# A three-set ring of routed rows, zeroed in long packets, with scatter waits per tile group and a rewritten order of steps

## The chip, the cores and the metric

The kernel runs on one NeuronCore of a Trainium2 chip. The metric is the device time of one execution in microseconds (us), lower is better. Engine names as in the profile: PE (TensorE matmul), PEld (its weight loads), DVE (VectorE), ACT (ScalarE), POOL (GpSimd), SP (SyncE, which issues most DMAs; SPq is its queue).

## The reference, cut to what matters

Four residual layers are applied to x of 8 batches x 1024 rows x 128 features, float32:

```
x = x + L0_attn(layernorm(x))   # "A": linear attention, a scan over the 1024 rows of a batch, 16 heads of 8x8 state
x = x + L0_ffn(layernorm(x))    # "B": mixture of 8 experts, 2 per row, hidden size 352
x = x + L1_attn(layernorm(x))   # "C": conv3 + selective state-space scan, 16 states per feature
x = x + L1_ffn(layernorm(x))    # "D": mixture of 8 experts, 2 per row, hidden size 128, and 2 shared experts
```

In both mixtures each row goes to its two best experts, and the two results are added with weights. A, B, C and D need nothing of another batch, so the batches form a pipeline.

## The kernel before, in words

All eight batches of x stay in SBUF. The scans of A and C run on VectorE: for a batch, A has 16 steps `a_outer` (L1454), `a_scan` (L1443), `a_qs` (L1461), and C has 16 steps `c_dbx` (L1511), `c_scan` (L1516), `c_prod` (L1502).

The mixtures are done in nine jobs: B0, B1, B23, B45, D01, B67, D23, D45, D6 (the letter is the layer, the digits are the batches; D of batch 7 is computed densely at the end). A job goes through these steps:

- Prepare: `m_stats`, `m_rstd` (POOL, L840), `m_shift`, and for each half batch (four tiles of 128 rows) `m_norm` (ACT, L1171, writes `xn`), `m_turn`, `m_turned`, `m_hi` (ACT, L1221, first half of the float16 split, writes `xrow`), `m_lo` (DVE, L1376), then `m_logits`, `m_choose`, `m_rank`, and `m_place` (DVE), which gives each row its two slots.
- `m_scatter` (POOL, L867): indirect DMAs, one for each tile of 128 rows and each of its two choices (c = 0, then c = 1), that write `xrow` to the job's row set in DRAM. 16 for a job of one batch, 32 for two.
- Blocks of 256 slots: SP loads the rows (`b_rows`, L750) and the experts' weights (`b_w13`, L732, and `b_w2`, L741), PE multiplies (L909 to L911, L1063), SP stores `outs` (L756).
- `m_gather` (POOL, L886): indirect DMAs that add the outputs into x, again one for each tile and choice.

The next layer's `s_stats` of a batch (or the end of the kernel) waits for its gathers, and `s_rstd` (also POOL, L840) follows on the same engine.

A row set has slots that no row is scattered to, and they are zeroed once, so each set is zeroed by a DMA (L686) from a zeroed tile before its first use. There are six sets, three for B and three for D, used in turn. The zeroed tile is the head of `xn`, so the first `m_norm` (L1188 to L1190) waits until all six sets and the float16 weights of B (`keep`, L717) are written. `m_hi` of a job waits in `all_scattered` for all scatters of all jobs before it, since the job before read the same tile `xrow`.

What each engine does in which order is a string ORDER of 4917 letters (L74). Each letter takes the next step of one chain (`chain`, L427): A the layer A, P preparation of jobs, X scatters, G gathers, C the layer C and its scalars, and so on. All engines run their own steps in this one order. Step numbers below are places in this string, from 0. The step `ready("C")` is the first of chain C. On PE and DVE and on ACT (L1163) it waits for the 13 loads of layer C's weights (L693 to L698).

SP's queue at the head issues, in order: x of batches 0 and 1, A's weights, the float32 expert weights (L677, L679), `zero("B", 0)`, x of batches 2 and 3, C's 13 weights, `zero("B", 1)`, `zero("B", 2)`, x of batches 4 to 7, D's weights, three zeroings for D, and then the steps of ORDER, `keep` first.

Of the kernel before, what the change touches and what calls it, by code (L numbers as in the profile page):

```python
# [13 lines left out]
P = 128  # L14
# [27 lines left out]
class BankUses:  # L42
# [56 lines left out]
    "NKkMGLVpdURVyocKqLxwGsAZbeVNhSZRSTRGMweUpeLqycVKoxwGsAehNeTZMeTqUGSMpRwLKoUVyxLKsGAhNeZeNVZpSRNGSTqZyRoMSsRe"
    "UCewLqGKCVsTCMCUqCwLKCGwTAMVTUoMsALKCUqNoLwVKZGCsACCqSoRwseCCGqNCwZVeCwSRPDGTCCMUCPCLKTCCGPMNPUVePCKLCPPCGCP"  # L100
    "ZCCNSPRCCeVCCPZGCSNPRPCCePPPGTMCPUBKTdPMdUccdbbLKLZNSRZPeNSZReVVNSPRZNSReZTSPMXRUTLMVTxUMNxXLbTZUVMbhNLSUKZX"
    "LVTdVNhSXMpZUdSNpKyLxXyZhccSbXVdxNehbZXSdXpPycpPycPxPhbPudxXlhbpdXvucplycxXyvbhnXnxdabhXpdpycXxcyhbXxdpbXhyc"
    "pdGxychbPRxdRGRPRbhPRPpPdGucPplyPcxyGvbhTnMTduxGhbMlTpUvcGpyLcxyhGnUaUVxMKULTGpLVyhUpNVyZeCSRUeCMKLTCCVUCGGG"
    "NCLGUZUSVRMKLTVUCNeLUGZCCUSVRCKCMGCTCUeLVCLGCCNCGCZeCCSRUCCVGCCUCCUCMKLCLVTCCBNCCCUUGVKUMeCLTccbdVbUddLZUVSN"
    "RMKLVPZxSNRPbheUZTSLURPdUKVMPLpTUexycLVbhNUPZpdUSRVycxKMhPUTbeLpdVycxhbNLUpdUVycKMLUxTehLbZSRVdpNcxyZhbSURUV"
    "dKpUMLyceLVPxNPPhbTZUSURVdKpPyxMcPhbTLUedVpUycLNxVUbZhSMKLTUVdURepLycxVUbhNMKLPZVdpuSRxcyPhbPleTPdvuNlpycZvS"
    "xRnhbneUadUpLycxVUbhUMKLTLVdpNcyxZShbURUMKVLTpxycVhNeUZUSLpUVyMKLxTVuhlevulpUvyLCUCCCUCNCMKLPZSVCeVnPPnCUaCU"
    "PCCCBNLeCUZCSLVPVCCPUCCLCCPXKUCCKCVCUCCNXCLKVCZCCSXKNCZCCSXKeXeCebdXbccedeXdXxhbPxdpGbhycPdpXPycxPhbPXudxlhb"
    "XpdpycXvcxyhbXnuxdXhlbpdXpycvcxyXhbnadxGhbpdRpPycGRPRxcPyRRhbPGPxduPhblTGpMdTPycvpMnGcyxTuhblGxdUvbpKnhUMGLy"
    "cKadTVpUNxGKyMLhTbMcLePVdxGVbUpZUehLyScKGLVNPZVNxSKZhNGZNSSpRRyxcRZRhGeSRpeyGeTMTUMGUpLKTLVyMVKCTGUMCLKVTUMC"  # L110
# [9 lines left out]
    "OJGFQIOJFQIGOJFQIOJGFQIOJFQGIOJFQIOGJFQIOJFQIOJFQGIOJOQQQ"  # L120
# [3 lines left out]
def build(nc, t, out):  # L124
# [36 lines left out]
    ROW_SETS = {"B": 3, "D": 3}  # L161
    NTH = [sum(j[0] == s for j in JOBS[:q]) for q, (s, _) in enumerate(JOBS)]
# [3 lines left out]
    with ctx:  # L166
# [45 lines left out]
        xs_d = {(s, i): dram(f"rows_{s}{i}", [SLOTS, D + 1], F32) for s in "BD" for i in range(ROW_SETS[s])}  # L212
# [75 lines left out]
        zero_rows = xn[:, :, :].rearrange("p j d -> p (j d)")[:, 0:D + 1]  # L288
# [29 lines left out]
        h_ring = [mix2[:, sh_at + i * U_WORDS:sh_at + (i + 1) * U_WORDS] for i in range(RH)]  # L318
        xg = sb("xg", [P, RX, NBT, D + 1])
# [22 lines left out]
        for n, (s, _) in KEEP.items():  # L342
            cols_kept = E * R[s]
            if n in stage_at:
                at = stage_at[n]
            stage[n] = arena_c[:, at:at + cols_kept]
            at += cols_kept
            kept[n] = [mix2[:, kept_at + i * cols_kept // 2:kept_at + (i + 1) * cols_kept // 2].bitcast(F16) for i in range(2)]
            kept_at += cols_kept

# [68 lines left out]
        def ssm(b):  # L419
# [13 lines left out]
                                     [("ready", "D")] * (JOBS[q][0] == "D" and NTH[q] == 0) + prepare(q)],  # L433
# [153 lines left out]
        s_zeroed = {key: sem(f"rows_zeroed_{key[0]}{key[1]}") for key in xs_d}  # L587
# [28 lines left out]
        scattered = sem("rows_scattered")  # L616
# [41 lines left out]
        def _(sp):  # L658
# [19 lines left out]
            for c, (r, rows) in enumerate(CHUNKS["B"]):  # L678
# [4 lines left out]
                         zero_rows[rows:P, 0:D].unsqueeze(1).broadcast_to([P - rows, E, D])).then_inc(s_kept["B"], 16)  # L683
# [15 lines left out]
            for i in range(1, ROW_SETS["B"]):  # L699
                zero("B", i)  # L700
# [1062 lines left out]
```

## Time and profile before

| | before |
|---|---|
| three executions | 1800.45, 1800.25, 1806.42 us, median 1800.45 |
| profiled execution | span 1833.6 us, 29178 instructions, mean clock 0.883 |
| PE busy | 1401.7 us (76% of the span) |
| DVE busy | 1361.4 us (74%) |
| ACT busy | 981.4 us (54%) |
| POOL busy | 929.9 us (51%) |
| chain that ended last | PE 23%, issue 16%, POOL 16%, DVE 15%, ACT 11%, SPq 9%, DMA 7% |
| DMA | 369.53 MB, mean 202 GB/s |

No other time of the profiled execution is given than its span. The span is 33.1 us over the median of the timed executions. Busy time is the time in which an engine executes. The "idle before" of an instruction is the time in which its engine stood idle just ahead of it, and the profile infers who ended that wait.

### The profile page before, as it was taken

To read this page: it belongs to the slowest core of one execution; us is meant where nothing else is said; L and a number is where in the kernel's file an instruction comes from. 1 tells how busy PE (TensorE), PEld (TensorE's weight loads), DVE (VectorE), ACT (ScalarE), POOL (GpSimd) and SP (SyncE) were. 2 spreads that over 40 slices of the span, in tenths; PEclk is the share of its full clock that TensorE was granted. 3 is DMA by queue.
4 is the path that set the end of the run, shared out by engine and by line. 5 is a ranking of instruction groups with operands and counts; after the bars stand their busy time and mean duration, and the time that the engine had idled before them with its cause. 6 is when DMAs were issued, how large, how long until landed. Compare 5 with 4: busy or idle time off the path is not lost.

```text
span 1833.6 us, 29178 instructions
## 1 busy us (share of the span) xinstructions
PE 1401.7 (76%) x9192; PEld 943.1 (51%) x9192; DVE 1361.4 (74%) x2543; ACT 981.4 (54%) x1663; POOL 929.9 (51%) x571
## 2 busy tenths in 40 slices
PE   6674899988999789688578567787836776767668
PEld 3342577755776556555355434565613553435345
DVE  6793969788997889649586588288759579639836
ACT  2213262638756666378264554677446575477332
POOL 1000422385451856828838588400278737852875
PEclk9886899999999999989889579889969788879879
DMA  9995373757884669858477678888468767876952
GB/s 238 162 184 116 90 208 119 212 137 249 281 263 137 215 218 292 230 145 281 148 213 169 185 231 220 231 291 281 125 200 247 200 202 250 225 209 210 287 111 50
DMA packets 320067, 369.53 MB, mean 202 GB/s; under 512 B 33801, under 2 KB 260521, under 8 KB 319657
## 3 DMA queue, kind: packets, MB, share of 16 engines
q1 hardware_dynamic: 277672, 336.05, 62.8%
q0 software_dynamic: 42240, 31.61, 9.6%
q8 instruction: 74, 1.21, 0.3%
q14 instruction: 81, 0.66, 0.1%
HBM read 306.09 MB, written 63.42 MB: 202 GB/s over the span
## 4 chain that ended last, share of the span: by engine, by line
PE 23%; issue 16%; POOL 16%; DVE 15%; ACT 11%; SPq 9%; DMA 7%; another core or an unknown queue 1%; POOLq 0%; DVEq 0%; ACTq 0%
POOL x L886 7%; POOL rows_D L867 5%; PE bank L991 3%; DVE arena_c L1516 3%; POOL rows_B L867 2%; PE bank L1063 2%; SPq L664 2%; SPq L686 2%; DVE arena_c L1502 2%; DMA x<-outs,slot_idx 2%; DMA arena_c<-bc_rows 2%; DVE arena_c L1511 2%; PE bank L1098 2%; DVE arena_a L1443 1%; PE bank L951 1%
## 5 line engine op out<-in xcount | busy, mean ns | idle before, releaser
L886 POOL DMA_INDIRECT x<-outs,slot_idx x240 | 465.4, 1939 | 205.2 <-issue 110.7
L991 PE MATMUL bank<-arena_c,ident 128*128 128x512 f32 x512 | 289.2, 702 | 96.9 <-DVE arena_c L1502 95.9
L1516 DVE TENSOR_TENSOR_SCAN arena_c<-arena_c 128x1024 f32<-128x1024 f32 x128 | 292.1, 2283 | 1.8
L909 PE MATMUL bank<-xT_ring,mix 128*128 128x128 f16 (+1 forms) x1296 | 240.9, 225 | 58.0 <-DVE mix L1688 16.7
L910 PE MATMUL bank<-xT_ring,mix 128*128 128x128 f16 (+1 forms) x1296 | 240.4, 225 | 0.0
L911 PE MATMUL bank<-xT_ring,mix 128*128 128x128 f16 (+1 forms) x1296 | 240.3, 225 | 0.0
L1063 PE MATMUL bank<-mix 128*128 128x128 f32 (+1 forms) x1296 | 192.2, 295 | 60.4 <-ACT yrow L1319 36.2
L1063 PEld LDWEIGHTS bank<-mix 128*128 128x128 f32 (+1 forms) x1296 | 172.9, 205 | 96.0 <-issue 86.0
L991 PEld LDWEIGHTS bank<-arena_c,ident 128*128 128x128 f32 x512 | 104.9, 222 | 218.9 <-DVE arena_c L1502 121.7
L867 POOL DMA_INDIRECT rows_D<-xrow,slot_idx x112 | 187.7, 1676 | 40.1 <-issue 30.1
L867 POOL DMA_INDIRECT rows_B<-xrow,slot_idx x128 | 182.2, 1423 | 46.0 <-issue 35.0
L1274 ACT ACTIVATE arena_c<-arena_c,A_w 128x1024 f32<-128x1024 f32 x128 | 145.2, 1147 | 84.2 <-DVE arena_c L1516 82.4
L909 PEld LDWEIGHTS bank<-xT_ring,mix 128*128 128x128 f16 (+1 forms) x1296 | 139.8, 108 | 91.5 <-issue 59.0
L942 PE MATMUL bank<-arena_a,Wv 128*128 128x512 f32 x256 | 148.9, 665 | 43.8 <-DVE arena_a L1454 30.0
L1319 ACT ACTIVATE yrow<-bank,xg 128x128 f32<-128x128 f32 x312 | 97.3, 364 | 135.3 <-PE bank L1063 116.5
L1511 DVE TENSOR_TENSOR arena_c<-arena_c 128x1024 f32<-128x1024 f32 x128 | 154.8, 1213 | 18.7 <-DMA arena_c<-bc_rows 18.7
L1502 DVE TENSOR_TENSOR arena_c<-arena_c 128x1024 f32<-128x1024 f32 x128 | 153.8, 1213 | 8.5 <-DMA arena_c<-bc_rows 8.0
L951 PEld LDWEIGHTS bank<-Wo,arena_a 128*128 128x128 f32 x1024 | 137.3, 205 | 39.9 <-issue 22.5
L1298 ACT COPY xT_ring<-bank 128x512 f16<-128x512 f16 x156 | 90.5, 580 | 114.4 <-PE bank L1038 64.9
L910 PEld LDWEIGHTS bank<-xT_ring,mix 128*128 128x128 f16 (+1 forms) x1296 | 139.5, 108 | 20.3 <-issue 19.7
L951 PE MATMUL bank<-Wo,arena_a 128*128 128x128 f32 x1024 | 143.2, 290 | 6.7 <-DVE arena_a L1461 6.3
L911 PEld LDWEIGHTS bank<-xT_ring,mix 128*128 128x128 f16 (+1 forms) x1296 | 139.6, 108 | 0.0
(225 smaller groups left out, 2460.4 us busy)
## 6 DMA issues: line engine op xcount, KB each, us to landing
arena_c<-bc_rows SPq DMA_DIRECT2D x256, 512.0 KB
mix<-weights_B SPq DMA_DIRECT2D x168, 352.0 KB
mix<-weights_B SPq DMA_DIRECT2D x168, 192.0 KB
outs<-yrow SPq DMA_DIRECT2D x156, 128.0 KB
mix<-weights_D SPq DMA_DIRECT2D x144, 128.0 KB
xg<-rows_B SPq DMA_DIRECT2D x84, 129.0 KB
xg<-rows_D SPq DMA_DIRECT2D x72, 129.0 KB
mix<-weights_D SPq DMA_DIRECT2D x144, 64.0 KB
```

Source lines behind the costliest of these rows:

```text
L867: pool.indirect_dma_start(out=xs_d[s, NTH[q] % ROW_SETS[s]], out_offset=bass.IndirectOffsetOnAxis(ap=slot_idx[:, q % RJ, c, j:j + 1], axis=0),
L886: pool.indirect_dma_start(out=x[:, b, j, :], out_offset=None, in_=y_d[q], in_offset=bass.IndirectOffsetOnAxis(ap=slot_idx[:, q % RJ, c, i ...
L909: pe.matmul(o, hi, xh, start=True, stop=False)
L910: pe.matmul(o, hi, xl, start=False, stop=False)
L911: return pe.matmul(o, lo, xh, start=False, stop=True)
L942: filled(f"A{b}.v{k}", pe.matmul(fill(f"A{b}.v{k}"), Wv[:, f, :], half(normA, h), start=True, stop=True))
L951: last = pe.matmul(bank[A_BANKS[1]][:, rows], qs[:, k % RQ, rows], Wo[:, f, :], start=(f == 0 and j == 0), stop=(f == EF - 1 and j == TH - 1))
L991: last = pe.matmul(bank[C_BANKS[h]][:], ident[:], half(hb[:, n % RR, :], h), start=(n == 0), stop=(n == NS - 1))
L1063: last = pe.matmul(o[:, j * P:(j + 1) * P], h_ring[n % RH][0:rows, at:at + P], w2(q, k, j)[0:rows, c, :], start=(c == 0), stop=(c == NC[s] ...
L1502: dve.tensor_tensor(hb[:, n % RR, :], hb[:, n % RR, :], Cb[:, g % RB, :], ALU.mult).then_inc(c_prod.sem, 1)
L1511: dve.tensor_tensor(hb[:, n % RR, :], Bb[:, g % RB, :], w, ALU.mult).then_inc(c_dBx.sem, 1)
L1516: dve.tensor_tensor_scan(hb[:, n % RR, :], dA[:, n % RDA, :], hb[:, n % RR, :], 0.0, ALU.mult, ALU.add).then_inc(c_scan.sem, 1)
```

## The change

1. One ring of three row sets for all jobs (job q uses set q mod 3) replaces three sets for B and three for D. Job q's scatters wait for the gathers of job q-3.
2. A set is zeroed by rows of 430 words (1720 bytes) that are contiguous in DRAM, from a tile of 128 x 430 words, instead of 516-byte rows. The zeroed tile is no longer the head of `xn` but the end of the third slot of the ring of hidden values. So the first `m_norm` waits for no zeroing, and the third unit's gate on DVE (`hidden_slot`) does, for all three sets and `keep` of B.
3. The second scatters (c = 1) count on one semaphore for each group of four tiles. `m_hi` waits for its own group's scatters of the jobs before, not for all.
4. ORDER is rewritten. The chains are the same, the interleaving is new.

```diff
-    ROW_SETS = {"B": 3, "D": 3}
+    ROW_SETS = 3
...
-        zero_rows = xn[:, :, :].rearrange("p j d -> p (j d)")[:, 0:D + 1]
+        SLOT_WORDS = SLOTS // P * (D + 1)
+        ZERO_WORDS = max(n for n in range(1, 513) if SLOT_WORDS % n == 0)
+        zeros = mix2[:, W_WORDS + (RS + RH) * U_WORDS - ZERO_WORDS:W_WORDS + (RS + RH) * U_WORDS]
...
-        scattered = sem("rows_scattered")
+        scattered_second = [sem(f"rows_scattered_second_{g}") for g in range(MT // TH)]
...
-        def all_scattered(w, q):
-            if q >= 0:
-                w.wait_ge(scattered, 16 * sum(JT[:q + 1]))
+        def all_scattered(w, q, groups=range(MT // TH)):
+            for g in groups:
+                if any(n > g * TH for n in JT[:q + 1]):
+                    w.wait_ge(scattered_second[g], 16 * TH * sum(n > g * TH for n in JT[:q + 1]))
...
-            def zero(s, i):
-                sp.dma_start(xs_d[s, i].rearrange("(n p) f -> p n f", p=P),
-                             zero_rows.unsqueeze(1).broadcast_to([P, SLOTS // P, D + 1])).then_inc(s_zeroed[s, i], 16)
-            zero("B", 0)
+            def zero(i):
+                sp.dma_start(xs_d[i].rearrange("(p r) f -> p (r f)", p=P).rearrange("p (n w) -> p n w", w=ZERO_WORDS),
+                             zeros.unsqueeze(1).broadcast_to([P, SLOT_WORDS // ZERO_WORDS, ZERO_WORDS])).then_inc(s_zeroed[i], 16)
+            zero(0)
...
-            for i in range(1, ROW_SETS["B"]):
-                zero("B", i)
+            for i in range(1, ROW_SETS):
+                zero(i)
...
-            for i in range(ROW_SETS["D"]):
-                zero("D", i)
...
-                    for r in range(q):
-                        if JOBS[r][0] == s and NTH[r] == NTH[q] - ROW_SETS[s]:
-                            job_gathered(wt, r)
+                    if q >= ROW_SETS:
+                        job_gathered(wt, q - ROW_SETS)
...
-                else:
-                    for key in xs_d:
-                        wt.wait_ge(s_zeroed[key], 16)
-                    wt.wait_ge(s_kept["B"], 16 * (4 + NC["B"] + 1))
...
             def m_hi(q, i, h):
-                all_scattered(wt, q - 1)
+                all_scattered(wt, q - 1, (i * NH + h,))
...
             def hidden_slot(n):
+                if n == RH - 1:
+                    for i in range(ROW_SETS):
+                        wt.wait_ge(s_zeroed[i], 16)
+                    wt.wait_ge(s_kept["B"], 16 * (4 + NC["B"] + 1))
```

Of the new ORDER, the head is `"AAAAPAAAACCAAAAAAAAAAAAAAAAWAAAA..."` where the old one is `"AAAAAAAAAPAAAAWAAAAAAAAAAAAWAAAo..."`. Places of some steps in the two strings:

| step | before | after |
|---|---|---|
| `ready("C")` | 84 | 9 |
| `s_turned("A", 0, 0)`, ACT's first read of A's first batch | 8 | 11 |
| the four `split` steps of the expert weights | 141, 151, 162, 165 | 86, 134, 136, 271 |
| `s_norm("A", 1)` | 130 | 137 |
| `m_norm(0, 0, 0)`, the first of job 0 (B0) | 246 | 159 |
| last `a_scan` of batch 1 | 260 | 257 |
| `m_place(0)` | 289 | 270 |
| `m_hi(4, 0, 0)` and the last scatter of job 3 | 1841 and 1807 | 1833 and 1809 |
| `s_rstd("C", 2)` and the gathers of batch 3 in job 2 | 2155, all 16 ahead of it | 2136, 4 of 16 ahead of it |
| `m_place(4)` | 2284 | 2265 |
| `m_norm(5, 0, 0)`, `m_hi(5, 0, 0)`, last scatter of job 4 | 2344, 2508, 2473 | 2366, 2446, 2439 |
| `b_turn(4, 0)`, the first block of job 4 on PE | 2556 | 2518 |
| `s_rstd("C", 3)`, the last gather of batch 3 in job 2 | 2736, 2140 | 2725, 2603 |
| `c_rate(5)`, the last `b_out_read` of job 5 | 3627, 3618 | 3616, 3674 |
| `s_rstd("C", 7)` and the gathers of batch 3 in job 6 | 4334, 8 of 16 ahead of it | 4319, none ahead of it |
| `d_rstd(7)` and the gathers of job 7 | 4762, 22 of 32 ahead of it | 4749, 20 of 32 ahead of it |

## Rows read from the trace of the kernel before

**Rows 1.** Timeline of SP's queue, head of the kernel: start us, us taken, what is issued.

```profile
26.23 0.45 SPq L686 DMA_DIRECT2D rows_B<-xn  x1
26.73 15.50 SPq L664 DMA_DIRECT2D x<-in_x  x2
52.63 11.13 SPq L686 DMA_DIRECT2D rows_B<-xn  x2
95.04 30.45 SPq L686 DMA_DIRECT2D rows_D<-xn  x3
125.62 24.47 SPq L717 DMA_DIRECT2D weights_B<-mix  x4
```

**Rows 2.** Waits 120:200 us: who waited for whom, us in total, times, longest.

```profile
ACT xn L1171 <- DMA weights_B<-mix: 38.6, 1, 38.6
DVE xrow L1376 <- ACT xrow L1221: 22.8, 2, 22.1
```

**Rows 3.** Stretches of the head: us, busy us by engine, granted clock, DMA share, GB/s.

```profile
13.30:80.70 67.40, 47.67 (x181) 27.60 (x180) 53.61 (x87) 8.40 (x21) 1.67 (x1) 0.86 1.05 191
80.70:95.80 15.10, 12.24 (x26) 4.16 (x26) 9.09 (x24) 13.19 (x19) 2.74 (x2) 0.84 1.17 214
95.80:138.80 43.00, 31.61 (x136) 19.50 (x134) 42.28 (x70) 3.71 (x11) 1.64 (x1) 0.88 1.26 172
125.00:145.00 20.00, 9.15 (x49) 6.23 (x47) 13.78 (x32) 0.00 (x0) 1.64 (x1) 0.88 1.29 163
148.00:156.00 8.00, 0.00 (x0) 0.00 (x0) 0.00 (x0) 0.00 (x0) 0.00 (x0) 0.50 1.16 303
```

**Rows 4.** Timeline of ScalarE and VectorE: start us, us, line, what [idle before].

```profile
13.28 1.25 ACT L1225 COPY arena_a<-bank 128x512 f32<-128x512 f32 x2
55.05 0.69 DVE L1422 TENSOR_TENSOR x<-bank,x 128x512 f32<-128x512 f32 x1 [6.26 <-DMA cols<-in_bbc]
84.27 2.64 ACT L1161 ACTIVATE mix<-arena_c,wscale 128x2816 f16<-128x2816 f32 x1
169.13 0.23 DVE L1542 TENSOR_REDUCE g_mx<-bank 128x8 f32<-128x64 f32 x1 [1.21 <-PE bank L1019]
185.21 0.68 DVE L1454 TENSOR_TENSOR arena_a<-bank,arena_a 128x512 f32<-128x512 f32 x1
```

**Rows 5.** Waits 655:680 us, part of a longer list.

```profile
DVE mix L1688 <- ACT mix L1310: 5.8, 1, 5.8
```

**Rows 6.** Waits 760:790 us.

```profile
DVE shift_C L1408 <- POOL rstd_C L840: 18.7, 1, 18.7
```

**Rows 7.** Timeline of GpSimd, 760:790 us, one of the last gathers ahead of rstd_C.

```profile
768.83 1.55 POOL L886 DMA_INDIRECT x<-outs,slot_idx  x1 [0.32 <-issue]
```

**Rows 8.** Waits 890:925 us.

```profile
ACT xrow L1221 <- DMA rows_D<-xrow,slot_idx: 24.8, 1, 24.8
DVE xrow L1376 <- ACT xrow L1221: 23.1, 1, 23.1
```

**Rows 9.** Scatters of L867 at 838:893.5, then at 897.5:917.6: ns min/median/max.

```profile
L867 POOL DMA_INDIRECT rows_D<-xrow,slot_idx x14: 1428/3656/6916, 838.1 to 887.5; - x14
L867 POOL DMA_INDIRECT rows_D<-xrow,slot_idx x16: 975/975/3181, 894.4 to 916.5; - x16
```

**Rows 10.** Timeline of GpSimd behind the scatters of job 4: its next instruction.

```profile
943.80 2.52 POOL L886 DMA_INDIRECT x<-outs,slot_idx  x1 [26.30 <-issue]
```

**Rows 11.** The same two stretches: us, busy us by engine, clock, DMA.

```profile
838.00:893.50 55.50, 50.67 (x298) 31.86 (x296) 55.50 (x58) 39.09 (x56) 51.40 (x15) 0.97 0.78 253
897.50:917.60 20.10, 1.00 (x3) 0.17 (x1) 0.00 (x0) 0.00 (x0) 14.94 (x17) 0.60 0.31 105
```

**Rows 12.** Waits 1600:1640 us, then 1740:1770 us.

```profile
DVE shift_C L1408 <- POOL rstd_C L840: 6.8, 1, 6.8
DVE arena_a L1408 <- POOL arena_a L840: 13.5, 1, 13.5
```

**Rows 13.** Timeline of VectorE at 1348 us.

```profile
1348.11 1.22 DVE L1493 TENSOR_TENSOR arena_c<-arena_c 128x1024 f32<-128x1024 f32 x1 [18.77 <-ACT arena_c L1265]
```

More of the change, by code:

```diff
@@ L120 @@
[L120 removed]
+    "AAAAPAAAACCAAAAAAAAAAAAAAAAWAAAAosAoAWoAqWksWosqWwAWoAqwkwssoqksAoAqWkoskwsAoqqwksAwokWsAqkWowqqsAowAqwwoAws"
+    "sowAqsoqAsqowqswwAAwqwAwPPWWWAAAAAAAAAAPAAAAAAAAAAAPAAoPAsoqAwsoqAwskkoWqsAPokqsAoPPwqPAoskkksAowwqAqowsAswo"
+    "qAkPkqoswsAowAqoPwwAsqoqsAPsqPowAAqwsAPoPsqwwPqCwAwPPwPWAAAAXAAAAAAPAWAAXAAAAAAAKAAAosAXoAskPoqAqokAKsoswkqA"
+    "oswXekXskAoqPPAqoweksskAwowXqAPqXPoswkAqPPoXAsPqPRwwoAswqwqPoswARowTsqMAqULUoTwswUMRVqLTRULsVRAUqUMToLNKAswq"
@@ new lines @@
+    "wZKVAPMVwNUUAwPATLUZVLAVMULRUeTUeMAALPARKVASCPKNSTPVAZUNAeUPALVUAAMPLAAUZAAVLPRUVAUAAALANPKVeARAAoKZUURLUKLT"
+    "AMNXVTUsLkVoAXqZMUsXoqsUAPwKwTXoMVskAoLUkSLqqAPeVoswsSRUUPqPAwXoLkVkkXwVAPsULUkoKTqAskwMUoAqNPsLwqoVZAVPeosU"
+    "wKAqNoAUsPPLwPRVUqowqSTLwAseMwZVqosUqANwossLXUqAAoXqRUwSeTZKwsPAMAqPRPLwPSwVNTKAVSwSAUUAePZLAVAUPeNMULARPVPP"
+    "ZLPUUPTASNPMPKZVPPSeUPKLPPSAVARPLUARVNPeeAUAKZLASATMAANPVGPZRAAeUPGLAUTULGNVMTAVARMAKZAUULUoLVAsoNeZGKkVqTAU"
+    "oswMRGLsRUkqAoNAVULsoZwVkqUTsLekAMUSUqKoVGwsGAoTLkwAUVULMUqwoKARLsGskVNqoASXZUTkMXVkwCLUoCUAqKswCqoLwVsCAoCC"
@@ new lines @@
+    "sqCXXUAVCSCCXosqCSLACCUqXCCsoCCURsCCCAKXTCCCXwXCeoSNeLAKCACwZwCCqwMqVVwXeswCAdNoZXURSUqTLqsdwMwqUbbVxwwAxAAc"
+    "AhAcNhpAXAZAXAepUdASNbALAKbLPAcAyAAxAVUhedxXAAXXZchbAAAUApLydPAbBKpRxocdcNyyhZVSdPAxTPVosMhRTbsRbkApRoUUSLeq"
+    "USxyMLsPwckVPUALVpqKTUNPULZoPVPbAMhexoyxVAPPeNpsqdcsRUTZPbUohKLUPALVxqMyPNVpUddPZTheLcoKURkSRNVUMsUTLhMbALke"
+    "GwoVdkqwUUxKwcqwpVGAeTLsUkVbGLowZGSqswKsUNkAGyMVdqhUGwoAUSykLswoxSbAZVpRLUKoVqqhsGecRUpTNZAMboLNweVydZAdUqss"
+    "UdoNAKLULRyqVoxTwAcMeVeUZKhTLxURMRpsodUANLySqwwwVqVTcsUSwMTKAUsqLAbpUVchZxewNULVUZbKqLSRUMwLypNAhAcVwARAAyAT"
@@ L121 @@
+    "SELEUEVKNeEZGLEGVNuZNlEvSZuTlNMEGZSEvULKERVnunlGTSaNvGeMuZnlSUvLnVaFNIJFZIJFEOIJOFIQJFQIOJQGOQFIOSJFQOIJQSFI"
+    "OJFIOJFQSIJFIQOJQFIJOFIQJOOFQIJFQOIJOFQIQJOQGOQGQGGGGGGGG"
 )
@@ L160, in build @@
     SLOTS = MOST_BLOCKS * NB
-    ROW_SETS = {"B": 3, "D": 3}
-    NTH = [sum(j[0] == s for j in JOBS[:q]) for q, (s, _) in enumerate(JOBS)]
+    ROW_SETS = 3
+    FIRST_OF = [next(q for q, j in enumerate(JOBS) if j[0] == s) for s, _ in JOBS]
     PARTS_UP_TO = [[sum(len(j[1]) > i for j in JOBS[:q + 1]) for i in range(MOST)] for q in range(len(JOBS))]
@@ L211, in build @@
         Wd = {s: dram(f"weights_{s}", [E, P, W13[s] + W2[s]], F32) for s in "BD"}
-        xs_d = {(s, i): dram(f"rows_{s}{i}", [SLOTS, D + 1], F32) for s in "BD" for i in range(ROW_SETS[s])}
+        xs_d = [dram(f"rows_{i}", [SLOTS, D + 1], F32) for i in range(ROW_SETS)]
         bc_d = [dram(f"bc_rows_{i}", [BC, T], F32) for i in range(2)]
@@ L349, in build @@
             kept_at += cols_kept
+        assert kept_at <= W_WORDS + (RS + RH) * U_WORDS - ZERO_WORDS and ZERO_WORDS <= U_WORDS
         g_lg, g_sel = (sb(f"g_{n}", [P, MT, E]) for n in ("lg", "sel"))
@@ L432, in build @@
             "P": [("ready", "B")] + [st for q in range(len(JOBS)) for st in
-                                     [("ready", "D")] * (JOBS[q][0] == "D" and NTH[q] == 0) + prepare(q)],
+                                     [("ready", "D")] * (JOBS[q][0] == "D" and FIRST_OF[q] == q) + prepare(q)],
             "X": [st for q in range(len(JOBS)) for st in scatters(q)],
@@ L586, in build @@
         s_kept = {s: sem(f"weights_kept_{s}") for s in "BD"}
-        s_zeroed = {key: sem(f"rows_zeroed_{key[0]}{key[1]}") for key in xs_d}
+        s_zeroed = [sem(f"rows_zeroed_{i}") for i in range(ROW_SETS)]
         x_in = [sem(f"x_loaded_{b}") for b in range(B)]
@@ L799, in _ @@
             pool.memset(neg_half[:], -0.5).then_inc(s_cons0, 1)
-            pool.memset(zero_rows, 0.0).then_inc(s_cons0, 1)
+            pool.memset(zeros, 0.0).then_inc(s_cons0, 1)
             wt.wait_ge(s_cons0, 3)
@@ L867, in m_scatter @@
                     pool.indirect_dma_start(
-                        out=xs_d[s, NTH[q] % ROW_SETS[s]], out_offset=bass.IndirectOffsetOnAxis(ap=slot_idx[:, q % RJ, c, j:j + 1], axis=0),
+                        out=xs_d[q % ROW_SETS], out_offset=bass.IndirectOffsetOnAxis(ap=slot_idx[:, q % RJ, c, j:j + 1], axis=0),
                         in_=xrow[:, j, :], in_offset=None, bounds_check=SLOTS - 1,
-                        oob_is_err=True).then_inc(scattered if c else scattered_first[j], 16)
+                        oob_is_err=True).then_inc(scattered_second[j // TH] if c else scattered_first[j], 16)
             def m_gather(q, i, c, first):
```

81 lines of the change are left out of this document (33 added, 48 removed).

## The prediction

> **What bounds the kernel now.** The table of the page comes first: PE is busy 76% and DVE 74% of the span, neither near full, so single waits matter. A search of the list of waits for those at which ACT, DVE and PE stand still together then gives the places where a change of order can pay. There are four long ones, and each is a wait for something slower than compute.
>
> At 119 to 157 us ACT stands at the first `m_norm` until the zeroings and `keep` have landed: 38.6 us on ACT, 22.8 us on DVE [rows 2]. SP's queue [rows 1] shows why: after B's first set, five more sets are zeroed (issues at 52.63 and 95.04) and `keep` goes out only at 125.62. Around 765 us DVE waits 18.7 us for `rstd_C`, which is queued on POOL behind gathers [rows 6, 7]. At 894 to 919 us ACT waits 24.8 us in `m_hi` for the scatters of job 4, DVE 23.1 us [rows 8]. At 1329 to 1348 us DVE waits 18.77 us for the serial front of layer C's fifth batch [rows 13]. Smaller ones: 5.8 us on DVE behind `m_hi` of job 4 [rows 5], 6.8 us behind `rstd_C` of batch 7 and 13.5 us behind `rstd` of the dense batch [rows 12]. Together that is 22.8 + 18.7 + 23.1 + 18.8 + 5.8 + 6.8 + 13.5 = 109.5 us of DVE, the most that this list could give back.
>
> **Change 2, the zeroing and the head.** Six sets of 2.64 MB become three, and `m_norm` waits for none. But the new order also moves `ready("C")` from step 84 to step 9, ahead of ACT's first read of batch 0 and of all attention on PE and DVE. That wait is no formality. Before, DVE stood 6.26 us at step 84 until the last C weight landed at 55.05 us [rows 4]. At step 9 attention of batch 0 cannot start until then, where it started at 13.28 us [rows 4].
>
> When do the C weights land? They are queued behind `zero(0)`. Zeroing in 516-byte rows moves 163 GB/s, and `keep`, whose rows are longer, 303 GB/s [rows 3]. One set at 163 takes 16.2 us, at 303 it takes 8.7 us, so I take 7.5 us off: 55.05 - 7.5 = 47.5 us. Bounds: 55.05 if length does not matter, 38.9 if `zero(0)` cost nothing.
>
> By the Trainium skill ("DMA: Bandwidth & Descriptors", Specifications) 512 bytes already suffice for line rate. By that rule the 516-byte rows were not slow for their length, and the landing stays at 55.05 us. The rows of `keep` against those of the zeroing speak against it, but they are no pure test, since the sources differ too. The head would then end 5 us late instead of 2 early, and my sum be 7 us smaller.
>
> From there by VectorE [rows 3, 4]. Attention of batch 0 took 13.3 to 80.7, 67.4 us. Less the wait of 6.3, with 0.5 for steps moved (an estimate: one peak of the weights in, C's small preparations out), that is 61.6. The front of batch 1 took 15.1 us; two splits of 2.64 us on ACT now stand ahead of it or before batch 0 ends, so 9.8. Its steps took 43.0; two small splits leave them, 40.6. The rest of batch 1 and `m_lo`, 7 us of work (an estimate from two steps of 2.6 us, two `m_lo`, one addition), runs without the stall, because job 0's `m_norm` now stands at step 159, inside batch 1. From the choice of experts (169.13) to the first step of batch 2 (185.21) nothing changes, 16.1. Sum: 47.5 + 61.6 + 9.8 + 40.6 + 7 + 16.1 = 182.6 against 185.2, a gain of 2.6; I take **2**. So the 22.8 us that go come back as a late start. Bounds: -5 (landing at 55.05) to +11 (38.9). The memset of the larger tile and the wait in `hidden_slot` cost nothing: three sets are done long before the third unit, as six were before.
>
> **Change 3, per-group waits.** For `m_hi` of job 5 only the first group of job 4's second scatters is needed. In the old order it stood at step 2508 behind the last scatter at 2473; all 16 second scatters came at 894.4 to 917.5 [rows 9], so ACT waited for the last of them. With group waits it would be free some four scatters in. That the 23.1 us vanish is not the whole of it. The 14 scatters at 838 to 893.5, with DVE busy 55.5 of 55.5 us, took 3656 ns in the median; the 16 in the stall, with DVE at zero, 975 ns [rows 9, 11]. If DVE works on, POOL writes them slowly. The 16 second scatters take 16 x 3.96 = 63 us (55.5 us over 14, from the same rows) instead of 23, and the blocks of job 4, all that PE had to take up, begin 40 us later relative to `m_place(4)`. DVE has the rest of batch 2 of C and batch 7 of A meanwhile. Bounds: +23.1 if DVE sets the pace, -17 if PE needs the blocks. I take **8**, a little above the middle, as C's scans are the longer work there. Job 4's own small wait (5.8 us [rows 5]): **4** of 0 to 5.8.
>
> The Trainium skill ("SBUF — State Buffer", SBUF: two separate sides) says that GpSimd cannot write descriptors while DVE holds the port pair that they share. The trace agrees on the direction with the 3656 and 975 ns; it cannot show the port. By that rule alone the gain here would be none.
>
> **Change 4, the order on POOL.** Before, all 16 gathers of batch 3 stood ahead of `s_rstd("C", 2)`, now 4 do: 12 gathers x (1.55 + 0.3) us = 22 us earlier on POOL [rows 7], more than the 18.7 us of the wait [rows 6]. The other 12 go behind job 4's scatters and are due at batch 3 of C, where POOL had 26.3 us idle [rows 10]. I take **15** of 0 to 18.7; the missing part is that the gathers left ran at 1.55 us only because DVE was idle. For batch 7 of C all 8 gathers ahead go behind: **6** of 0 to 6.8. For the dense batch 20 instead of 22 stand ahead, 2 x 1.85 = 3.7: **3** [rows 12]. The front of C's fifth batch [rows 13] now has job 5's last block behind it (3674 against 3618), but PE, not DVE, gets that work: **0**, of 0 to 18.8.
>
> **Change 1.** One ring of three adds waits for gathers of job q-3. On POOL these gathers are issued ahead of those scatters in the new order for every q, and `m_place` already waited for q-4. The nearest case is job 4 for job 1: those gathers end at step 1525 and the scatters begin at 2289. No cost.
>
> **The rest of the order** I cannot price: every chain is interleaved anew. Its bounds are from repeated waits: +30 (the long wait of rows 13 and the fillers close) to -30 (new waits of the size of those in rows 6 and 13). I take zero.
>
> **Sum:** 2 + 8 + 4 + 15 + 6 + 3 = 38 us of the profiled 1833.6. Scaled by 1800.45/1833.6 it is 37, so **1763 us**.
>
> **Rivals.**
>
> - A, *the head eats the gain* (slower). If the C weights land at 55.05 us, batch 0 starts 41.8 us late, and only DVE's stall and its own wait, 22.8 + 6.3, come back: the head is 12.7 us late. This holds if job 0's preparation inside batch 1 stretches batch 1 as much as it did outside. The later waits then are shorter by themselves, since what they wait for (scatters, gathers) starts from DMAs of the head that are not late, and give nothing more. Price: 1800 + 13 = **1813**. It decides when the landing is past about 50 us and the later terms stay under 5 us. For it: `ready("C")` is a plain wait on three engines, and its row is there. Against: rows 6 and 8 are queue effects on POOL, whatever the head does.
> - B, *scatters and gathers stretch*. POOL's slowness under a busy DVE takes the terms of job 4 and batch 2 of C: 8 becomes -10 and 15 becomes 5. Sum 38 - 18 - 10 = 10, so **1790**. For it: 3656 against 975 ns. Against: POOL is busy 51% only.
> - C, *the order closes more*. The wait of 18.8 us at C's fifth batch and small ones go too, 38 + 30 = 68, scaled 67: **1734**. For it: DVE's waits above sum to 109.5 us. Against: PE has little ready work at those places.
> - D, *the zeroing is not faster at all* and the new order was chosen for something else: the head is 5 late, 31 remains, **1770**. It is inside the forecast's own range, 1745 to 1785.
>
> **Chances.** Forecast with D 0.48, B 0.20, C 0.18, A 0.14. What can be told from no change here is about 0.5%, 9 us: 1791.4 to 1809.5. All of the forecast and C and half of B and more are faster: 0.78. Same: part of B and of A, 0.09. Slower: the rest of A and what is unpriced in the order, 0.13. The range takes in B and C and the near side of A: 1728 to 1810.
>
> **What the profile after would show.** Right: DVE nearly idle from about 12 us until the last C weight lands, near 47 us; the wait of ACT for `weights_B` at the first `m_norm` gone; the first step of batch 2 of A near 183; no wait of over 10 us behind `rstd_C` of batch 2; `m_hi` of job 5 without a wait for `rows`, and scatters of job 4 all at 2 to 5 us. Wrong: a landing near 55 with the head 10 us late; new waits of PE over 15 us for `xg` after a job's scatters (B); a span under 1775 (C).

## The result, and the profile after

The kernel after takes **1756 us** (median of 4 runs, 1748 to 1762) against 1803 us before; the ratio is 0.9726, 95% interval 0.9689 to 0.9763. The forecast was 1763 us. The gain is 47 us by the runs, 76 us by the two profiled spans. The span before (1833.6 us) was a long one of its kernel, so traces are used below to say where time went, and ratios to say how much.

The table of the page after: PE rises from 76 to 79%, DVE from 74 to 78%.

```profile
span 1757.8 us, 29149 instructions
PE 1386.4 (79%) x9192; PEld 950.4 (54%) x9192; DVE 1364.6 (78%) x2543; ACT 957.4 (54%) x1652; POOL 945.7 (54%) x571
```

The next two views are the stretches of before and after (columns as in [rows 3], the engines in the order PE, PEld, DVE, ACT, POOL), cut where POOL starts `rstd` of the first D batch, of C's batch 3 and of C's batch 6. Before:

```profile
0.00:600.00 600.00, 497.67 (x3436) 342.75 (x3436) 478.24 (x1050) 278.34 (x536) 191.78 (x150) 0.92 0.73 183
600.00:985.30 385.30, 301.00 (x2234) 212.02 (x2232) 297.84 (x461) 227.75 (x362) 254.91 (x123) 0.91 0.73 217
985.30:1451.90 466.60, 329.98 (x2029) 215.75 (x2028) 332.37 (x542) 270.39 (x414) 254.42 (x160) 0.84 0.76 221
1451.90:1833.60 381.70, 273.02 (x1496) 172.61 (x1496) 252.97 (x492) 204.94 (x353) 228.83 (x141) 0.85 0.69 192
```

After:

```profile
0.00:599.30 599.30, 491.55 (x3495) 343.39 (x3496) 483.69 (x1062) 279.45 (x544) 208.67 (x157) 0.96 0.59 174
599.30:945.00 345.70, 294.84 (x2169) 212.93 (x2167) 293.03 (x447) 192.58 (x331) 233.15 (x116) 0.93 0.79 231
945.00:1381.40 436.40, 324.64 (x2028) 220.75 (x2028) 332.30 (x544) 272.58 (x419) 252.35 (x149) 0.84 0.81 234
1381.40:1757.80 376.40, 275.32 (x1504) 173.29 (x1504) 255.60 (x491) 212.79 (x360) 251.52 (x152) 0.85 0.74 199
```

DVE is busy for nearly the same time in each stretch; what shrinks is its idle time. Between these two traces the first third of the kernel gains nothing (600.0 against 599.3 us), the second stretch 39.6 us, the third 30.2. Part of that is the long trace of before: in `e5_group_only` below, which has the order of before, a head with the same waits and a span of 1811.3 us, the first D batch's `rstd` starts at 584.7 us. Against that trace the kernel after is 15 us late at this point, so all of its gain comes later.

The head, from the waits and VectorE's timeline after:

```profile
DVE arena_c L1466 <- DMA cols<-in_bbc: 34.9, 1, 34.9
47.87 0.68 DVE L1466 TENSOR_SCALAR arena_c<-ident,convw_w 128x128 f32<-128x128 f32 x3 [34.88 <-DMA cols<-in_bbc]
192.11 0.68 DVE L1451 TENSOR_TENSOR arena_a<-bank,arena_a 128x512 f32<-128x512 f32 x1
```

The last C weight lands at 47.87 us, where [rows 4] had 55.05. The wait of ACT for `weights_B` [rows 2] is gone. But the first step of batch 2 of A comes at 192.11, not at 185.21 [rows 4]: later, not earlier. Of the waits behind `rstd`, that of [rows 6] is down from 18.7 to 1.4 us, and those of [rows 12] from 6.8 and 13.5 to 3.5 and 3.3. The one of [rows 8] is now, in the waits of 850 to 880 us:

```profile
DVE xrow L1373 <- ACT xrow L1218: 4.6, 2, 2.9
ACT xrow L1218 <- DMA rows<-xrow,slot_idx: 3.4, 1, 3.4
```

The wait at the front of C's batch 5, 18.77 us in [rows 13], is nearly gone too:

```profile
1282.22 1.22 DVE L1490 TENSOR_TENSOR arena_c<-arena_c 128x1024 f32<-128x1024 f32 x1 [1.55 <-ACT arena_c L1262]
```

### The profile page after: what moved, and what is told of

The parts are those of the page before. It is cut to its first block, busy times and chain, and to the rows that moved or that the text cites. A ratio compares the mean times of both kernels' runs of the same rounds, so it can differ in the third digit from the quotient of the medians.

```text
span 1757.8 us, 29149 instructions
## 1 busy us (share of the span) xinstructions
PE 1386.4 (79%) x9192; PEld 950.4 (54%) x9192; DVE 1364.6 (78%) x2543; ACT 957.4 (54%) x1652; POOL 945.7 (54%) x571
## 4 chain that ended last, share of the span: by engine, by line
PE 39%; issue 13%; DVE 13%; POOL 12%; DMA 9%; ACT 8%; SPq 4%; POOLq 0%; DVEq 0%; ACTq 0%
POOL rows L868 7%; PE bank L1064 5%; PE bank L992 5%; POOL x L887 4%; PE bank L943 4%; PE bank L952 3%; DMA rows<-xrow,slot_idx 3%; DMA x<-outs,slot_idx 3%; PE bank L910 3%; PE bank L938 2%; DVE arena_a L1440 2%; PE bank L912 2%; PE bank L911 2%; DVE arena_a L1458 1%; PE bank L1099 1%
## 5 line engine op out<-in xcount | busy, mean ns | idle before, releaser
L868 POOL DMA_INDIRECT rows<-xrow,slot_idx x240 | 369.1, 1538 | 85.7 <-issue 61.3
L910 PE MATMUL bank<-xT_ring,mix 128*128 128x128 f16 (+1 forms) x1296 | 252.2, 231 | 65.2 <-DVE mix L1689 25.5
L992 PE MATMUL bank<-arena_c,ident 128*128 128x512 f32 x512 | 263.9, 648 | 25.6 <-DVE arena_c L1499 25.6
L911 PE MATMUL bank<-xT_ring,mix 128*128 128x128 f16 (+1 forms) x1296 | 251.2, 230 | 0.0
L912 PE MATMUL bank<-xT_ring,mix 128*128 128x128 f16 (+1 forms) x1296 | 250.9, 230 | 0.0
L1064 PEld LDWEIGHTS bank<-mix 128*128 128x128 f32 (+1 forms) x1296 | 177.0, 208 | 75.1 <-issue 74.1
L910 PEld LDWEIGHTS bank<-xT_ring,mix 128*128 128x128 f16 (+1 forms) x1296 | 144.0, 111 | 106.6 <-issue 59.7
L1508 DVE TENSOR_TENSOR arena_c<-arena_c 128x1024 f32<-128x1024 f32 x128 | 156.0, 1222 | 16.8 <-DMA arena_c<-bc_rows 8.9
L1499 DVE TENSOR_TENSOR arena_c<-arena_c 128x1024 f32<-128x1024 f32 x128 | 157.3, 1233 | 9.5 <-DMA arena_c<-bc_rows 8.8
L992 PEld LDWEIGHTS bank<-arena_c,ident 128*128 128x128 f32 x512 | 98.5, 208 | 117.9 <-issue 86.3
L952 PEld LDWEIGHTS bank<-Wo,arena_a 128*128 128x128 f32 x1024 | 135.5, 204 | 37.2 <-issue 19.8
L911 PEld LDWEIGHTS bank<-xT_ring,mix 128*128 128x128 f16 (+1 forms) x1296 | 143.4, 111 | 21.6 <-issue 20.3
L912 PEld LDWEIGHTS bank<-xT_ring,mix 128*128 128x128 f16 (+1 forms) x1296 | 143.7, 111 | 0.0
L1307 ACT ACTIVATE mix<-bank,winv 96x256 f32<-96x256 f32 (+1 forms) x156 | 73.0, 472 | 99.1 <-PE bank L912 97.0
```

The lines of the kernel that those rows point to most:

```text
L868: pool.indirect_dma_start(out=xs_d[q % ROW_SETS], out_offset=bass.IndirectOffsetOnAxis(ap=slot_idx[:, q % RJ, c, j:j + 1], axis=0), in_=xr ...
L910: pe.matmul(o, hi, xh, start=True, stop=False)
L911: pe.matmul(o, hi, xl, start=False, stop=False)
L912: return pe.matmul(o, lo, xh, start=False, stop=True)
L952: last = pe.matmul(bank[A_BANKS[1]][:, rows], qs[:, k % RQ, rows], Wo[:, f, :], start=(f == 0 and j == 0), stop=(f == EF - 1 and j == TH - 1))
L992: last = pe.matmul(bank[C_BANKS[h]][:], ident[:], half(hb[:, n % RR, :], h), start=(n == 0), stop=(n == NS - 1))
```

## The experiments

Each expectation was written before its run; it names a theory and one or more rivals.

All ratios are to the kernel before, run beside them on the same chip; 1% is 18 us. `e1` to `e4`, `e5` to `e8` and `e9` to `e12` each shared their runs of before; the kernel after (0.9726) had its own, so it and the experiments are compared by their ratios.

### The change in two halves: e1 and e2

`e1_order_only` is the kernel before with the new string `ORDER` and nothing else:

```diff
 ORDER = (
-    "AAAAAAAAAPAAAAWAAAAAAAAAAAAWAAAoWAsokqAswokqAswokqAswokq...
+    "AAAAPAAAACCAAAAAAAAAAAAAAAAWAAAAosAoAWoAqWksWosqWwAWoAqw...
```

> The kernel before with the new order of steps alone: six row sets, zeroing in 516-byte rows, m_norm waiting for all of it, m_hi waiting for all 16 scatters. Theory (the order carries the queue terms of 24 us, the code the rest): the C weights land at 55 us again, so the head is some 7 us later than in the kernel after, and m_norm of job 0 waits up to 10 us more for the zeroings; m_hi of job 5 gives back 8. About 1780 us (1770 to 1795), which is 1 to 2% under the kernel before. Rival (nearly all of the gain is the order, the head's late start costs nothing later): 1760. Rival (the order was fitted to the new waits and loses without them): 1800 or more.

`e2_code_only` is the reverse: all of the change but `ORDER`.

> The kernel after with the old order of steps: one ring of three sets, long packets, per-group waits, m_norm without the wait for the zeroings. Theory: the stall of 22.8 us and the wait of 6.3 us in the head go, m_hi of jobs 4 and 5 give 12, the waits behind rstd_C (18.7, 6.8, 13.5 us) stay: some 1760 to 1770. Rival (what the head gains is lost again by the next wait that ends on a DMA or on POOL): 1785 to 1800.

Measured: e1 **1.0132** (1.0107 to 1.0157), e2 **0.9867** (0.9825 to 0.9909). The order alone costs 24 us, the code alone gains 24, and both together gain 49. So 49 us of the result belong to neither half alone. For e1 the rival "loses without them" held; for e2 the 24 us lie between theory and rival.

That e1 is slower does not mean that the whole order loses without the new waits. VectorE's wait for C's weights, now at step 9, is 43.1 us in e1, where before it was 6.26 [rows 4]:

```profile
DVE arena_c L1469 <- DMA cols<-in_bbc: 43.1, 1, 43.1
```

The difference is 37 us. If all of it is on the path, as e3 below found for the kernel after, the rest of the order gains about 13 us even in e1 (an estimate; no run has it).

### C's weights: e3, e7, e8

`e3_c_late` is the kernel after, with `ready("C")` and `conv_taps` at steps 83 and 84:

```diff
-    "AAAAPAAAACCAAAAAAAAAAAAAAAAWAAAAosAoAWoAqWksWosqWwAWoAqwkwssoqksAoAqWkoskwsAoqqwksAwokWsAqkWowqqsAowAqwwoAws"
+    "AAAAPAAAAAAAAAAAAAAAAAAAAWAAAAosAoAWoAqWksWosqWwAWoAqwkwssoqksAoAqWkoskwsAoqqwksAwoCCkWsAqkWowqqsAowAqwwoAws"
```

> The kernel after, with ready(C) and conv_taps moved from steps 9 and 10 back to steps 83 and 84, nothing else. Theory (all three engines stand until 47.9 us for weights that nobody needs before step 84, and what follows is bound by compute): the first outer product comes at 13 instead of 48 us, the whole run is 25 to 35 us shorter, 1721 to 1731 us. Rival (the late start is cover for transfers of the head, the zeroings and keep, and the gain is given back at the first wait for them or behind the POOL queue): 1745 to 1756.

`e7_zero_short` is the kernel after with 516-byte rows from the same tile of zeros:

```diff
-                sp.dma_start(xs_d[i].rearrange("(p r) f -> p (r f)", p=P).rearrange("p (n w) -> p n w", w=ZERO_WORDS),
-                             zeros.unsqueeze(1).broadcast_to([P, SLOT_WORDS // ZERO_WORDS, ZERO_WORDS])).then_inc(s_zeroed[i], 16)
+                sp.dma_start(xs_d[i].rearrange("(n p) f -> p n f", p=P),
+                             zeros[:, 0:D + 1].unsqueeze(1).broadcast_to([P, SLOTS // P, D + 1])).then_inc(s_zeroed[i], 16)
```

> The kernel after with its three sets zeroed in 516-byte rows from the same tile of zeros. Theory (the length of the packets sets the time of a zeroing, 16.2 against 8.7 us): the last C weight lands at about 55 us instead of 47.9, all engines start 7 us later and the run is 7 us longer, ratio 0.977. Rival (512 bytes are long enough, length does nothing): landing at 48, ratio 0.973.

`e8_weights_first` issues C's weights ahead of every zeroing:

```diff
-            zero(0)
             load_x(2)
...
-            for i in range(1, ROW_SETS):
+            for i in range(ROW_SETS):
                 zero(i)
```

> The kernel after with zero(0) put behind the loads of C's weights on SP, so that ready(C) at step 9 waits for less. Theory (the wait at ready(C) is on the path at its full length): the weights land at 38 to 40 us instead of 47.9, and the run is 8 to 10 us shorter, ratio 0.967 to 0.968. Rival (DMAs of the head other than zero(0) hold the weights up): 0 to 3 us, ratio 0.971 to 0.973.

Measured: e3 **0.9530** (0.9504 to 0.9555), 1726 us, 35 us under the kernel after and the fastest of all; its theory held. e7 0.9794 (0.9761 to 0.9827), e8 0.9680 (0.9645 to 0.9714). VectorE's wait for the last of C's weights, of e7, then of e8:

```profile
DVE arena_c L1466 <- DMA cols<-in_bbc: 41.9, 1, 41.9
```

```profile
DVE arena_c L1465 <- DMA cols<-in_bbc: 25.9, 1, 25.9
```

With the 34.9 us of after, that is 7.0 us more for short rows and 9.0 less when the weights go first. The runs move by 12 and 8 us, with intervals of about 9 us either way, so e8 by itself does not exclude its rival of 0 to 3 us. Held against each other, e7 and e8 (one chip, the same runs of before) differ by 21 us, 12 to 29, for 16.0 us of waiting. With the 35 us of e3 for a wait of 34.9, that puts the full length of this wait on the path, as the theories had it. The three sets take 13.0 us in the median from issue to landing after, 19.8 us in e7. (Such medians compare only at the same places in the queue: in e8, which issues the same long rows for all three sets at once, it is 19.2 us.) The Trainium skill ("DMA: Bandwidth & Descriptors", Specifications) puts the minimum transfer for line rate at 512 bytes; here the 516-byte rows were slower than 1720-byte ones from one source tile, so the measurement decides against its use in this place. The edit also changes which partition writes which rows of the set in DRAM; no run separates that from the length of the rows.

### The group waits: e4 and e5

`e4_wait_all` takes the per-group waits out of the kernel after; `e5_group_only` puts them alone into the kernel before (its six zeroings then share one semaphore):

```diff
             def m_hi(q, i, h):
-                all_scattered(wt, q - 1, (i * NH + h,))
+                all_scattered(wt, q - 1)
```

> The kernel after, with m_hi of every job waiting again for all scatters of the job before. Theory by the prediction (per-group waits are worth 8 us at job 5 and 4 at job 4): 1756 + 12 = 1768 us. Rival (the new order puts m_hi of job 5 only 7 steps behind the last scatter, so that the wait is short, and for jobs 1 to 4 it stands behind them all): 1756 to 1760 us, no difference that can be told.

> The kernel before with the per-group waits of m_hi alone (the six zeroings counted by one semaphore, all of them awaited as before): old order, six sets, short packets. Theory (in the old order only job 5's m_hi, and a little of job 4's, stand in front of open scatters; the new order opened four such waits of 17 to 20 us and so made the group waits worth some 43 us): 10 to 20 us less than before, ratio 0.989 to 0.995. Rival (group waits are worth the same in any order): 40 us less, ratio 0.976.

Measured: e4 **0.9962** (0.9941 to 0.9982), 43 us slower than the kernel after; both theory (12 us) and rival (none) fell far short. e5 **0.9990** (0.9968 to 1.0012), 2 us, less than its theory's 10 to 20. The same edit is worth 43 us in one order (35 to 51) and 2 us, give or take 4, in the other. So this edit alone accounts for some 41 of the 49 us that belong to neither half. The waits of e4 show why. Windows around 660, 880, 1070 and 1355 us, for jobs 4, 5, 6 and 7:

```profile
ACT xrow L1218 <- DMA rows<-xrow,slot_idx: 18.3, 1, 18.3
...
ACT xrow L1218 <- DMA rows<-xrow,slot_idx: 18.9, 1, 18.9
DVE xrow L1373 <- ACT xrow L1218: 18.4, 1, 18.4
...
ACT xrow L1218 <- DMA rows<-xrow,slot_idx: 20.3, 1, 20.3
DVE xrow L1373 <- ACT xrow L1218: 15.3, 1, 15.3
...
ACT xrow L1218 <- DMA rows<-xrow,slot_idx: 16.7, 1, 16.7
DVE xrow L1373 <- ACT xrow L1218: 11.5, 1, 11.5
```

Four waits of ACT of 17 to 20 us, where before there was the one of 24.8 [rows 8] and one of 9.3 at job 4: the new order sets `m_hi` close behind the scatters, or ahead of the last of them (job 6 at step 2991, last scatters at 2996 to 3005). With group waits the last three are 3.4, 4.1 and 3.3 us and the first is gone. Over the whole kernel VectorE waits 70.2 us for `xrow` in e4 and 26.2 us after, and the 44 us between them are the size of what the runs show.

In e5 job 5's wait shrank from 23.1 to 7.4 us on DVE, and the runs did not move. PE's waits show where it went. In the waits of 890 to 925 us of before, PE stood for job 5's rows:

```profile
PE bank L1011 <- ACT xn L1171: 24.1, 1, 24.1
```

In those of 860 to 960 us of e5 it stands for them for a third of that, and then for the rows of job 4's blocks (`xg`), for which the trace of before has no such wait there:

```profile
PE bank L1012 <- ACT xn L1172: 8.4, 1, 8.4
PE bank L1039 <- DMA xg<-rows_D: 13.3, 3, 7.1
```

Together 21.7 us for 24.1. That is the mechanism of the prediction's rival B, in the old order. After, the new order has 1.3 us of `xg` waits at this place. This is read from the traces, not tested.

### Where the order gains: e6, e9, e10, e11

`e6_pool_order` starts from e2. It moves 12 gathers of batch 3 in job 2 behind `s_rstd(C,2)`, and 8 gathers of batch 3 in job 6 behind `s_rstd(C,7)` (its expectation calls them gathers of batch 7); `e11_gathers_back` moves the 12 of batch 3 back ahead of it in e3. As edits of the list of steps:

```diff
 # e6, old order
-m_gather(2,1,0,4..6) m_gather(2,1,1,0..6) ... s_rstd(C,2) ... m_scatter(4,1,14)
+s_rstd(C,2) ... m_gather(2,1,0,4..6) ... m_scatter(4,1,14) m_gather(2,1,1,0..6)
-m_gather(6,1,0,0..6) ... s_rstd(C,7) m_rstd(8,0)
+s_rstd(C,7) m_rstd(8,0) m_gather(6,1,0,0..6)
 # e11, order of e3
-s_stats(C,2) s_rstd(C,2) ... m_gather(2,1,0,4..6) ... m_gather(2,1,1,0..6)
+m_gather(2,1,0,4..6) m_gather(2,1,1,0..6) ... s_stats(C,2) s_rstd(C,2)
```

> The code of the kernel after with the old order (e2_code_only, ratio 0.9867), in which 12 gathers of batch 3 are moved behind s_rstd of C's batch 2 (four to a later place ahead of job 4's scatters, eight behind them), and 8 gathers of batch 7 behind s_rstd of C's batch 7. Theory of the prediction (the waits of 19.0 and 7.0 us go, 15 and 6 us of it last): 21 us under e2, ratio 0.975. Rival (POOL and DVE have the same gathers to do later and give most of it back, and the new order's gain of about 60 us between e2 and e3 comes from how its chains are interleaved): 0 to 8 us, ratio 0.983 to 0.987.

> e3_c_late with the 12 gathers of batch 3 that stand behind s_rstd of C's batch 2 put back ahead of its statistics. Theory of the prediction (this place on POOL is worth 15 us): ratio 0.953 + 0.008 = 0.961. Rival from e6 (the wait opens by 15 to 19 us at 720 us and is won back behind it, since the same gathers no longer stand between job 4's scatters and C's batch 3): 0 to 5 us, ratio 0.953 to 0.956.

Measured: e6 0.9849 (0.9814 to 0.9884), 3 us under e2; e11 0.9601 (0.9574 to 0.9628), **13 us** over e3. The waits on `rstd_C` around 740 us, of e2 (none in e6) and then of e11 (none in e3):

```profile
DVE shift_C L1405 <- POOL rstd_C L842: 19.0, 1, 19.0
```

```profile
DVE shift_C L1405 <- POOL rstd_C L842: 13.2, 1, 13.2
```

For e11 the theory held by the runs: 13 us, 6 to 20, from a wait of 13.2. By the two traces the lead of e3 is 14.7 us at C's batch 3 and only 3.9 at the end, but the traced run of e3 is the slowest of its six. For e6 the rival held. In e6 the 19 us were gained (C's batch 2 began at 732.6 instead of 752.7 us) and then lost: C's batch 6 began only 6 us earlier (its own wait behind `rstd_C` is 9.5 us, for 2.0 in e2), and the lead of 15 us regained at batch 7 was gone at the end. A new wait of DVE for `bc_rows` stands there, in the waits of 1565 to 1590 us of e6:

```profile
PE bank L1064 <- ACT yrow L1316: 11.7, 1, 11.7
DVE arena_c L1508 <- DMA arena_c<-bc_rows: 11.0, 1, 11.0
```

`e9_new_then_old` and `e10_old_then_new` cut the two orders at `s_rstd(C,2)`: the steps of one up to and with it, then all that are left in the sequence of the other. In the old order it is step 2155; the expectation of e10 gives a wrong number.

```diff
-ORDER = order_of_e3
+ORDER = order_of_e3[0:2137] + what is left, as in the old order      # e9
+ORDER = old_order[0:2156] + what is left, as in the order of e3      # e10
```

> The order of e3_c_late up to s_rstd of C's batch 2 (its steps 0 to 2136), then the steps that are left in the old order; code of the kernel after. Theory (the order's gain over e2_code_only, 61 us, lies where the traces of e2 and e3 part: 35 of 46 us before the start of C's batch 2): about 35 to 45 us under e2, ratio 0.962 to 0.967. Rival (a lead won early is given back behind it, as that of e6 was): 0 to 15 us under e2, ratio 0.979 to 0.987.

> The complement: the old order up to s_rstd of C's batch 2 (step 2149), then what is left in the order of e3_c_late; code of the kernel after. Theory (as for e9): 15 to 25 us under e2, ratio 0.973 to 0.978. Rival (the second part holds the gain): 45 to 60 us under e2, ratio 0.954 to 0.962.

Measured: e9 0.9854 (0.9825 to 0.9882), e10 0.9707 (0.9673 to 0.9740). Against e2 that is 2 and 29 us, where the whole order gives 61; the halves do not add up. Part of the reason is seen at the seam. Each half, set before the other, leaves a `rstd` behind POOL's queue. Waits around 740 us, of e9, then of e10:

```profile
DVE shift_D L1405 <- POOL rstd_D L842: 20.4, 1, 20.4
```

```profile
DVE shift_A L1405 <- POOL rstd_A L842: 21.7, 1, 21.7
```

The wait of [rows 6] did not go; it moved to whichever normalisation was next. e9's theory missed by 33 us and its rival held; e10 came out 4 us under the lower end of its theory.

How the whole order clears this stage, e2 against e3, from `rstd_D` of the first D batch to `rstd_C` of batch 3 (of e2, then of e3):

```profile
564.60:949.00 384.40, 304.14 (x2225) 214.99 (x2223) 297.63 (x460) 226.64 (x360) 259.01 (x124) 0.90 0.72 217
```

```profile
567.80:911.90 344.10, 292.51 (x2169) 211.26 (x2167) 293.81 (x447) 193.04 (x331) 235.93 (x116) 0.95 0.78 232
```

40 us less for nearly the same work of DVE. Of these, 19.0 are the wait above; another 12.8 are one that the prediction never priced, in e2 at 625 to 650 us, where PE waits for the rows of job 3's first block, and DVE behind it:

```profile
PE bank L1039 <- DMA xg<-rows: 14.0, 1, 14.0
DVE mix L1689 <- ACT mix L1307: 12.8, 1, 12.8
```

In e3 `mix` L1689 waits 3.8 us in the whole stage, against 27.2 us in e2. PE's busy time is lower too, by 11.6 us, at a granted clock of 0.95 for 0.90. Whether the higher clock is part of the cause or comes of there being fewer stops was not tested; over the whole span it is 0.901 in e3 and 0.895 in e2.

### The ring: e12

`e12_six_sets` is the kernel after with a ring of six (one semaphore counts their zeroings):

```diff
-    ROW_SETS = 3
+    ROW_SETS = 6
```

> The kernel after with six row sets in place of three, all in long packets (one semaphore counts the six). Theory (the ring itself costs nothing, the weights of C wait only for the first set): landing at 48, ratio 0.973 as the kernel after. Rival (the three more zeroings, 26 us of transfers, delay x and the weights of the experts and job 0): 5 to 15 us slower, ratio 0.976 to 0.981.

Measured: 0.9728 (0.9697 to 0.9759), the same as the kernel after; VectorE's wait for C's weights is 34.8 us. Within 9 us, half as many sets gain nothing and a ring of three costs nothing; the lower end of the rival (5 us) is not excluded.

## Why the prediction came out right, and where it was wrong

The time was 7 us off. Its direction and the waits that it named were right, but the size was luck in part: terms that were too high and too low cancelled.

- **Landing of C's weights.** 47.5 forecast, 47.87 measured, and the 7.5 us for packet length measured as 7.0 by e7. That the wait at step 9 is no formality was right too, and e3 prices it: 35 us.
- **Head.** +2 forecast; batch 2 of A came 7 us later than in the trace of before, below the bound of -5. The failed term is "the front of batch 1 took 15.1 us; two splits ... stand ahead of it, so 9.8", with the 0.5 for steps moved. From the landing to the first outer product of batch 1 (129.7 us) were 82 us, where the terms have 74; before it was 79 without the wait of 6.3. The moved splits saved nothing: in e3, which has them too, batch 1 starts at 94.88, in e2, with the old places, at 92.41. And the stall of [rows 2] was a long one: in e5, with the same head, ACT's wait was 31.4 us and batch 2 began at 176.69, so against that run the head is 15 us late. The zeroing edits are worth 22 us in the old order (e5 to e2).
- **Group waits, 8 + 4 = 12.** Measured 2 us in the old order (the term, taken from a place near the middle of -17 to +23, was too high) and 43 us in the new one. The step that failed is the one that sized the term by [rows 8]: the waits were read from the trace of before, though the edit's worth depends on the waits that the new order would open without it. That the vanished wait can come back as late blocks was priced, and in the old order it did. Steps 2943 to 3005 and 3662 to 3690 could have been held against `m_hi` of jobs 6 and 7 as well, as the prediction did for job 5.
- **POOL's order, 15 + 6 + 3 = 24.** The 15 us hold in the order of e3 (13 by e11), and next to nothing of 15 + 6 holds in the old one (3 by e6, uncertain by 10 to either side). The price of a queue edit was right where the order behind it could use the lead. A reading was wrong: of the 12 gathers only 8 go behind job 4's scatters, 4 stand ahead of them (steps 2216 and 2288). Over the whole kernel VectorE's waits behind `rstd_C` and the dense batch's `rstd` go from 38.4 and 13.5 us in e2 to 18.4 and 1.6 in e3. That is 32 us of waiting, and more than the 24 forecast.
- **The front of C's batch 5 [rows 13], 0 of 0 to 18.8.** This wait closed to 1.55 us. With the old order it is 9.03 us in e2 and in e5, so some 7 us of it are the order's; the step that failed is "PE, not DVE, gets that work".
- **The rest of the order, 0 of -30 to +30.** The largest miss. Without the early `ready("C")` the new order is worth 61 us with the new code (e2 to e3), where the prediction had 24 for POOL and 0 for the rest. Put in its own groups, the measured sum is: head 22 - 35 = -13 (for +2), group waits 2 (for 12), order 61 (for 24), together 50 for 38. Two terms were too high by 15 and 10, one too low by 37. This sum takes the group waits at their worth in the old order; the other 41 us of them lie in the 61. Taken last instead, they are 43, and the order about 20 (an estimate from e4, e3, e2 and e5). Either way the term that is missing is what the order and the waits give only together. Rival C, "the order closes more", had the mechanism and, in the wait of [rows 13], one of the places.
- **Rival A** was right on its place: at the first D batch the head had eaten its whole gain (599.3 us, against 600.0 in the trace of before and 584.7 in that of e5). It was wrong that nothing came later.
- **Rival B.** The 16 second scatters of job 4 in the kernel after, at 846.5 to 877.3 us, and that stretch:

```profile
L868 POOL DMA_INDIRECT rows<-xrow,slot_idx x16: 967/1418/2782, 847.6 to 875.5; - x16
846.50:877.30 30.80, 23.13 (x129) 15.54 (x128) 23.82 (x26) 16.86 (x23) 24.81 (x18) 0.89 0.66 208
```

  31 us, not 63: with DVE busy 77% of the stretch the median is 1418 ns, between the 975 and 3656 ns of [rows 9]. They stretch, but much less than priced, and PE has no wait of over 15 us for `xg`. The Trainium skill ("SBUF — State Buffer", SBUF: two separate sides) has GpSimd locked out of the shared port pair, and so from writing descriptors, while DVE runs an operation of the kind that takes the pair. The three medians agree on the direction, and no run here shows the port.
- **Ring, 0.** Right within 9 us (e12).
- **The signs.** The landing, the wait for `weights_B` and the one behind `rstd_C` came as forecast. Batch 2 of A was to start near 183 and started at 192; `m_hi` of job 5 was to have no wait and has 3.4 us; job 4's second scatters were to take 2 to 5 us and take 1.4 in the median. The span of 1757.8 us also met the sign set for rival C, under 1775, which was set from a span of before that was itself 33 us long.

What stays open: why e6's lead was lost again is read from its trace, not tested; and of the 61 us about 50 are pinned to places by waits of DVE that shrink (32 behind `rstd`, 12.8 behind job 3's rows, 7 at [rows 13]), not by runs that change one of them. Only the 12 gathers were tested by themselves (e11).

## What to carry to other kernels

Price a relaxed wait against the order that it will run in: list, for each place, the steps of the new order on both sides of it. An order fitted to new waits and those waits are one change; each alone tells the wrong sign or size (order alone +24 us, in which the early `ready("C")` weighs most, group waits alone -2, the whole -49). And before a fitted order is kept, look for plain waits at its very front: two letters moved 74 places were worth 35 us.

## What the hardware showed

Zeroing in rows of 516 bytes against 1720 bytes, from one tile and at the same places in the queue: 19.8 against 13.0 us from issue to landing, and 7.0 us in the wait for what is queued behind the first of them (e7, after). A `rstd` on POOL behind a dozen gathers or more let DVE wait 13 to 22 us in four different orders (e2, e9, e10, e11).
